# 24 of the 98 dense pairs placed beneath the final scatter, which waits for stored pairs once in seven chunks

## The reference

```python
def _egnn_conv(x, src, dst, edge_attr, W_msg, W_edge, W_root, b):
    msg = x[src] @ W_msg + edge_attr @ W_edge
    agg = jax.ops.segment_max(msg, dst, num_segments=x.shape[0])
    agg = jnp.where(jnp.isneginf(agg), 0.0, agg)
    return agg + x @ W_root + b
...
c1 = leaky_relu(_egnn_conv(X,  src, dst, edge_attr, W1_msg, W1_edge, W1_root, b1))
c2 = leaky_relu(_egnn_conv(c1, src, dst, edge_attr, W2_msg, W2_edge, W2_root, b2))
out = layernorm(x + c2)
```

## Time and profile before

| | |
|---|---|
| time, median of 2 runs | 1471.7 us (1471.67 to 1471.73) |
| the profiled execution's own time | 1473.16 us |
| its span | 1471.4 us |
| mean granted TensorE clock | 0.712 of 2.4 GHz |
| TensorE busy | 1008.0 us, 69% |
| VectorE busy | 803.4 us, 55% |
| ScalarE busy | 699.0 us, 48% |
| GpSimd busy | 989.6 us, 67% |

### The profile page before, as it was taken

The page is one execution under the profiler, slowest core; times in us unless marked ns, Lnnn a source line. Parts: engine busy times, 40 slices in busy tenths (PEclk is TensorE's granted clock), DMA queues, the critical chain, the costliest instruction groups (busy, mean ns, idle before and its releaser), DMA issues.

```text
span 1471.4 us, 16389 instructions
## 1 busy us (share of the span) xinstructions
PE 1008.0 (69%) x4312; PEld 665.1 (45%) x4312; DVE 803.4 (55%) x1736; ACT 699.0 (48%) x1711; POOL 989.6 (67%) x986
## 2 busy tenths in 40 slices
PE   3667677779999999988988898989898940000000
PEld 1333333346666666665655666656666630000000
DVE  3223332357777777777877888888888850000000
ACT  1223343346666666656666666666666660000000
POOL 4777777757777776467676767677765007777775
PEclk9787787785555555598988888889888865555555
DMA  7888798877776777666665666655666211111110
GB/s 208 258 271 271 210 293 286 273 223 219 206 219 202 218 205 216 207 186 174 168 168 166 168 172 176 171 165 153 178 175 170 86 41 34 34 34 32 34 34 26
DMA packets 106083, 247.72 MB, mean 168 GB/s; under 512 B 26664, under 2 KB 27729, under 8 KB 105992
## 3 DMA queue, kind: packets, MB, share of 16 engines
q1 hardware_dynamic: 67432, 161.21, 36.5%
q0 software_dynamic: 31360, 47.07, 13.7%
q10 hardware_dynamic: 7200, 38.40, 6.9%
HBM read 141.94 MB, written 105.80 MB: 168 GB/s over the span
## 4 chain that ended last, share of the span: by engine, by line
PE 35%; POOL 22%; issue 19%; DVE 11%; ACT 11%; DMA 1%; DVEq 0%; POOLq 0%; ACTq 0%; SPq 0%
PE ps L408 13%; PE ps_z L418 13%; POOL g_src L229 12%; POOL out L248 8%; ACT yo L555 5%; DVE yo L720 3%; PE ps_m L398 3%; DVE stat L731 3%; PE ps_t L394 2%; ACT c1d L640 2%; DVE rt L822 2%; POOL g_dst L229 2%; ACT nat L617 2%; PE ps_r L504 2%; PE ps_r L506 1%
## 5 line engine op out<-in xcount | busy, mean ns | idle before, releaser
L418 PEld LDWEIGHTS ps_z<-wr,c1t 97*128 97x128 f32 x1568 | 296.4, 272 | 103.3 <-issue 72.9
L408 PE MATMUL ps<-xtb,wr 97*96 97x512 f32 x392 | 300.4, 861 | 0.0
L418 PE MATMUL ps_z<-wr,c1t 97*128 97x96 f32 x1568 | 293.7, 352 | 2.9 <-DVE c1t L713 2.9
L248 POOL DMA_INDIRECT out<-nat,end_i x196 | 190.5, 972 | 136.6 <-DMA out<-yo 75.8
L229 POOL DMA_INDIRECT g_src<-agg_table,src_i x196 | 214.8, 1096 | 84.5 <-issue 54.3
L229 POOL DMA_INDIRECT g_dst<-in_x,own_i x196 | 189.2, 965 | 106.8 <-DVE nat L802 57.4
L239 POOL DMA_INDIRECT agg_table<-nat,all_i x196 | 206.3, 1053 | 72.9 <-issue 58.4
L555 ACT ACTIVATE yo<-yo,shift,rstd 128x96 f32<-128x96 f32 x680 | 253.0, 456 | 0.0
L229 POOL DMA_INDIRECT g_src<-in_x,src_i x196 | 188.0, 959 | 71.6 <-issue 58.8
L678 DVE TENSOR_TENSOR_SCAN mx<-mask,mx,ps_m 96x512 f32<-96x512 f32 x96 | 122.2, 1273 | 164.8 <-PE ps_m L398 164.8
L713 DVE TENSOR_TENSOR c1t<-ps,c1t 96x512 f32<-96x512 f32 x196 | 134.1, 684 | 75.0 <-ACT c1t L529 73.7
(11 more groups left out here) (57 smaller groups left out, 1172.5 us busy)
## 6 DMA issues: line engine op xcount, KB each, us to landing
xtb<-in_xt SPq DMA_DIRECT2D x98, 384.0 KB, 5.0
agg_table<-zero ACTq DMA_DIRECT2D x50, 750.0 KB
xn<-in_x SPq DMA_DIRECT2D x97, 384.0 KB, 3.3
out<-yo SPq DMA_DIRECT2D x97, 384.0 KB, 3.9
mask<-mask_row SPq DMA_DIRECT2D x98, 192.0 KB, 5.7
root_keep<-rt SPq DMA_DIRECT2D x49, 192.0 KB, 4.9
rt<-root_keep SPq DMA_DIRECT2D x49, 192.0 KB, 4.5
xe<-in_eat SPq DMA_DIRECT2D x98, 64.0 KB, 4.8
```

The lines of the kernel that those rows point to most:

```text
L248: nc.gpsimd.indirect_dma_start(out=rows, out_offset=bass.IndirectOffsetOnAxis(ap=end_i[:, t:t + 1], axis=0), in_=nat[:, t, :], in_offset=N ...
L408: nc.tensor.matmul(ps_1[0:D, h, :], wr1[:, :], xtb[:, k, half(h)], start=True, stop=True).then_inc(d_1, 1)
L418: last = nc.tensor.matmul(ps_z[:, h, row(j)], c1t[:, q % 2, cols(h * HJ + j)], wr2[:, :], start=True, stop=True)
```

## The change

- The 98 pairs are distributed anew: 6 in stage A as before, 35 in stage S (46 before), 33 in stage B (46 before), and 24 (`LATE` = 74 and up) in new loops behind stage B, on every engine that takes part. The late pairs normalise two of eight row blocks on VectorE.
- GpSimd no longer waits for all stores ahead of the final scatter. Once in GROUP = 7 chunks it loads a value from the last row of `pair_i` into a register: the number of pairs that must be stored so that all rows to which these seven chunks go are stored. It waits for the semaphore `s_stored` against that register.
- SyncE counts stored pairs into `s_stored`: after issuing the store of pair q it waits for the store of pair q - 1 to land and increments.
- The final scatter has no bounds check. It uses the index list of the table's scatter, which sends rows that are not a segment's last to rows of their own behind the output; `out` gets EP = 25088 more rows, cut off afterwards. `all_i` and the old `end_i` become one list, so one preparing operation goes (L657) and two are added for `pair_i`. GpSimd's start now waits for ten preparing operations, not nine.

```diff
-NS = 46
+NS = 35
+NM = 33
+GROUP = 7
...
-STEPS_B = spread(NQ - NA - NS, NCH, NA + NS)
+STEPS_B = spread(NM, NCH, NA + NS)
+LATE = NA + NS + NM
+STEPS_B[NCH] = range(LATE, LATE + 1)
+STEPS_B[NCH + 1] = range(LATE + 1, LATE + 2)
...
         def on_vector(q):
-            return VROWS if q < NA + NS else 0
+            return VROWS if q < NA + NS or q >= LATE else 0
...
             def scatter(rows, c, landed):
...
                         out=rows, out_offset=bass.IndirectOffsetOnAxis(ap=end_i[:, t:t + 1], axis=0),
-                        in_=nat[:, t, :], in_offset=None, bounds_check=N - 1,
-                        oob_is_err=False).then_inc(landed[c % 2], 16)
+                        in_=nat[:, t, :], in_offset=None).then_inc(landed[c % 2], 16)
...
-            pool.wait_ge(s_prep, 9)
+            pool.wait_ge(s_prep, 10)
...
-                scatter_maxima(c)
+                scatter(table, c, sc_t)
...
-            for k in range(YR):
-                pool.wait_ge(o_st[k], 16 * ((NQ + YR - 1 - k) // YR))
             for c in range(NCH):
+                if c % GROUP == 0:
+                    last = (c + GROUP) * TPC - 1
+                    pool.wait_ge(s_stored, nc.gpsimd.value_load(pair_i[P - 1:P, last:last + 1], min_val=1, max_val=NQ))
+                    pool.sem_inc(s_under, 1)
+                    pool.wait_ge(s_under, c // GROUP + 1)
                 pool.wait_ge(e_done, c + 1)
                 scatter(out, c, sc_o)
...
                 else:
                     sp.dma_start(out_tail, yo[0:TAIL, k, :]).then_inc(o_st[k], 16)
+                if q >= 1:
+                    stored(q - 1)
+
+            def stored(q):
+                sp.wait_ge(o_st[q % YR], 16 * (q // YR) + 16)
+                sp.sem_inc(s_stored, 1)
...
-            dense(range(NQ, NQ + 3))
+            dense(range(LATE, NQ + 3))
+            stored(NQ - 1)
...
                     last.then_inc(b_r, 1)
+            for d in range(LATE + 1, NQ + 1):
+                for h in range(2):
+                    dense(range(d, d + 1), h)
...
+            for d in range(LATE + 2, NQ + 2):
+                dense_head(range(d, d + 1))
+                dense_tail(range(d, d + 1))
             act.wait_ge(s_cleared, 16 * NZ)
...
-            V.scalar_tensor_tensor(out=end_i[:, :], in0=eq_c[:, :], scalar=float(FAR), in1=dst_i[:, :],
-                                   op0=ALU.mult, op1=ALU.add).then_inc(s_prep, 1)
...
+            V.tensor_scalar(pair_i[:, :], own_i[:, :], PN.bit_length() - 1, None,
+                            ALU.arith_shift_right).then_inc(s_prep, 1)
             dve.wait_ge(s_prep, 8)
-            V.tensor_tensor(all_i[:, :], aside_d[:, :], dst_i[:, :], ALU.add).then_inc(s_prep, 1)
+            V.tensor_tensor(end_i[:, :], aside_d[:, :], dst_i[:, :], ALU.add).then_inc(s_prep, 1)
+            V.tensor_scalar(pair_i[:, :], pair_i[:, :], 1, None, ALU.add).then_inc(s_prep, 1)
...
                 dense_tail(steps)
+            for d in range(LATE + 2, NQ + 2):
+                dense_head(range(d, d + 1))
+                dense_mid(range(d, d + 1))
+                dense_tail(range(d, d + 1))
```

More of the change, by code:

```diff
@@ L28 @@
 NA = 6
-NS = 46
+NS = 35
+NM = 33
 VROWS = 2
 AHEAD = 4
+GROUP = 7
+assert NCH % GROUP == 0
 assert N * D % (P * ZCOL) == 0 and NZ == NCH + 1 and NQ == 2 * NCH and (N - (NQ - 1) * PN) % J == 0
@@ L90, in gnn_kernel @@
         end_i = sb("end_i", [P, NT], i32)
-        all_i = sb("all_i", [P, NT], i32)
+        pair_i = sb("pair_i", [P, NT], i32)
         aside_i = sb("aside_i", [P, NT], i32)
@@ L151, in gnn_kernel @@
         o_st = sems("o_st", YR)
+        s_stored = sem("s_stored")
+        s_under = sem("s_under")
         sc_t = sems("sc_t", 2)
@@ L232, in gather @@
                     ).then_inc(landed[k], 16)
[L234 to L241, removed]
             def scatter(rows, c, landed):
@@ L348, in _ @@
             load_pair(1)
-            sp.wait_ge(s_prep, 9)
+            sp.wait_ge(s_prep, 10)
             sp.dma_start(mask_row, row_m[:, :]).then_inc(s_mask_w, 16)
@@ L482, in _ @@
                 else:
-                    dense(range(NQ, NQ + 1), 0)
-                    dense(range(NQ, NQ + 1), 1)
+                    dense(STEPS_B[c], 0)
+                    dense(STEPS_B[c], 1)
                 if c >= 1:
@@ L623, in _ @@
                     edge_std(c - 2)
-                steps = STEPS_B[c] if c < NCH else range(NQ + c - NCH, NQ + c - NCH + 1)
+                steps = STEPS_B[c]
                 dense_head(steps)
@@ L656, in _ @@
             V.tensor_scalar(row_m[:, :], row_m[:, :], 2.0, -1.0, ALU.mult, ALU.add).then_inc(s_prep, 1)
-            V.scalar_tensor_tensor(out=end_i[:, :], in0=eq_c[:, :], scalar=float(FAR), in1=dst_i[:, :],
-                                   op0=ALU.mult, op1=ALU.add).then_inc(s_prep, 1)
             V.tensor_scalar(own_i[:, :], dst_i[:, :], float(N - 1), None, ALU.min).then_inc(s_prep, 1)
             V.tensor_tensor(aside_d[:, :], aside_i[:, :], dst_i[:, :], ALU.subtract).then_inc(s_prep, 1)
-            dve.wait_ge(s_prep, 6)
+            dve.wait_ge(s_prep, 5)
             V.tensor_scalar(row_m[:, :], row_m[:, :], FMAX, None, ALU.mult).then_inc(s_prep, 1)
             V.tensor_tensor(aside_d[:, :], aside_d[:, :], eq_c[:, :], ALU.mult).then_inc(s_prep, 1)
+            V.tensor_scalar(pair_i[:, :], own_i[:, :], PN.bit_length() - 1, None,
+                            ALU.arith_shift_right).then_inc(s_prep, 1)
             dve.wait_ge(s_prep, 8)
-            V.tensor_tensor(all_i[:, :], aside_d[:, :], dst_i[:, :], ALU.add).then_inc(s_prep, 1)
+            V.tensor_tensor(end_i[:, :], aside_d[:, :], dst_i[:, :], ALU.add).then_inc(s_prep, 1)
+            V.tensor_scalar(pair_i[:, :], pair_i[:, :], 1, None, ALU.add).then_inc(s_prep, 1)
             dve.wait_ge(s_const, 9 * 16)
@@ L878 @@
         args[name] = nc.dram_tensor(f"in_{name}", a.shape, mybir.dt.from_np(a.dtype), kind="ExternalInput").ap()
-    out = nc.dram_tensor("out_0", (N, D), mybir.dt.float32, kind="ExternalOutput").ap()
+    out = nc.dram_tensor("out_0", (N + EP, D), mybir.dt.float32, kind="ExternalOutput").ap()
     gnn_kernel(nc, **args, out=out)
-    return run_bass_kernel_spmd(nc, [feed], core_ids=[0]).results[0]["out_0"]
+    return run_bass_kernel_spmd(nc, [feed], core_ids=[0]).results[0]["out_0"][0:N]
```

## The result

The changed kernel takes 1329.0 us (median of 2 runs, 1328.58 to 1329.41) against 1471.7: a ratio of 0.903, 95% interval 0.899 to 0.907. Four more runs of it beside the experiments gave 1328.6 us. The prediction was 1337 us, range 1320 to 1372.

The account below looks back on a forecast made before the run. GpSimd's list of indirect DMAs was taken to bind stages S, B and the final scatter: scatter start 1061 + 247 DMAs + 13 holds + 7 register waits + 8.5 end = 1336.5, plus 0.3, so 1337 us, range 1320 to 1372.

Parts of the forecast that it names:

- Stage S: 35 pairs instead of 46: GpSimd's scatter binds, first gather of stage B at 582.1, chunk 0 on VectorE at 591.
- Stage B: GpSimd's 360 gathers outlast the engines' list by 12 us; with 3 us of waits the final scatter starts at 1061.
- The term for VectorE's hold: In stage B, VectorE's work lengthens GpSimd's gathers by 0.85 us a pair, 28 us for 33 pairs.
- The 3 us for interlocking lists: In stage B, 3 us added for waits of GpSimd's list and the engines' list for one another.
- The engines' list: Stage B's 32 chunk intervals with a pair and 16 without: 492 us, so chunk 48 starts at 1083.
- The final scatter: Behind stage B: 196 DMAs of 1.26 us, 247 us, plus 13 us of losses beneath pairs and 7 of register waits.
- register waits: In the final scatter, seven register loads and waits on GpSimd cost 1.0 us each, 7 us.
- Group 6: Final scatter's group needing all 98 pairs: starts at 1292, no wait by 15 us; rival that it waits: 1364 us, chance 0.05.
- the prediction's estimate of 50 us by that page: In the final scatter, an exclusive port lock would charge 2.1 us for each of 24 late pairs; sum 1377.
- the lists did not interlock: Rival, stage B: GpSimd has no lead, chunks without a pair last 10.3 us, not 6.87; end at 1377, chance 0.14.
- The late pairs did not run at full clock: Rival, final scatter: late pairs take 5.03 us and cost GpSimd 1.24 each, +20, 1357 us; chance 0.12.
- Stage B's clock: Rival: TensorE's clock falls in stage B, at 1.2 GHz throughout 1577 us; chance 0.04.

Follow-up runs that it names:

- the early clears: The changed kernel with the clears of the table issued four chunks earlier on ScalarE's queue: 1319.4 us, ratio 0.897.

## Why the prediction was right, step by step

**The bound.** Right in mechanism. GpSimd's list of indirect DMAs binds from stage S on. It waits for nothing in stage B, the scatter follows the last gather at 0.30 us, and the early clears moved the end by what they took out of the list.

**Stage S.** First gather at 580.2 (582.1 predicted), chunk 0 on VectorE at 587.7 (591). The landing behind the last scatter DMA took 1.5 us instead of 3.9.

**Stage B.** The last gather ended at 1050.7 and the scatter started at 1051.0, where 1061 was predicted. That is the whole error of the sum: 1336.8 us for a span of 1326.5. The time was missed by only 8 us because a second error stood against it: the prediction put 0.3 us between span and time, from the span of one run and the median of two, but a run takes 1.7 to 2.2 us more than its own span (1473.16 and 1471.4 before, 1328.58 and 1326.5 after). The term for VectorE's hold was 28 us; 361.1 us for 360 gathers at 0.944 leave 21. The 3 us for interlocking lists were not needed. A loss per pair was the wrong unit besides: the kernel with 21 pairs in stage B lost 19.6 us and that with 40 pairs 28.4. Put down to the operation that ends 0.81 to 0.85 us ahead of each lengthened DMA, the 21 us of the changed kernel are 11.3 for the 33 pairs and 10.0 for the chunks' own L817 and L797; with 21 pairs it is 12.7 and 6.8, so 12 fewer pairs saved nothing there. The engines' list was sized well: chunk 48 at 1088.4 (1083).

**The final scatter.** 266.9 us, where 267 was predicted, but from other parts, so that the sum came out was luck. Predicted: 247 of bare DMAs, 13 of holds (10 beneath the late pairs, 3 ahead of them), 7 of register waits. Measured: 247, and 204.7 - 196 x 0.958 = 17 of holds (11.6 beneath the late pairs, 5.3 ahead of them), 0 of register waits, 3 of the odd gap. The late pairs ran at 6.72 us after the first few, as forecast, at a granted clock of 0.53, and then cost 0.41 us each. But the additions of the last pair of stage B and of the first three late ones came 5.1 to 7.5 us apart and cost 1.0 to 1.34 us each, the dearest above the 1.24 of the earlier trace rows. What a hold costs depends on where in the addition the DMA starts. At 6.72 us the two keep in step: from the start of an addition to that of the fifth DMA behind the held one it is 0.94 + 0.83 + 0.30 + 4 x 1.26 = 7.1 us, about 0.4 us into the next addition, where the held DMAs of the earlier trace rows start too. That is an estimate from these rows; it gives the 0.4 us a pair again.

**Group 6.** The last store was issued at 1269.6 and counted as landed at 1272.1, and group 6 started at 1282.8, as in this row, without a wait:

```profile
1282.82 0.96 POOL L247 DMA_INDIRECT out<-nat,end_i  x1 [0.30 <-issue]
```

Predicted: landed at 1277, start at 1292. The slack of 15 us is some 11, and 12 more late pairs used it up and more.

**Wrong in it.** The step "VectorE's L720 and L731, 2.1 us together, lengthen the scatter DMA" (lines of the kernel before). Of the two only the addition, L720, does. The Trainium skill ("SBUF — State Buffer", on the shared port pair) excludes a VectorE operation with at most one SBUF input from the contention, outside the 2-port modes, so the prediction's estimate of 50 us by that page should not have counted the statistics. With the addition alone it would have been 24 x 0.94 = 23 us; 11.6 were measured beneath the late pairs. And the register waits were put at 7 us and cost nothing.

**The rivals.** Chunks without a pair took 7.1 to 8.4 us, not 10.3: the lists did not interlock. The late pairs did not run at full clock (granted 0.53, with TensorE busy for 165 of 175 us). Group 6 didn't wait. Stage B's clock was 0.88 up to the last gather, not lower than before but a little higher.

## What to carry to other kernels

When one engine's list of DMAs runs through all stages, add up that list alone, from its first wait to its last issue, and look at what it waits for; other engines' work costs only where it makes that list wait or slows its instructions. A coarse wait at the end ("all stores") and a split of work that is to hide beneath it belong together: here the finer wait alone gained 80 us, the split alone lost 60, and both gained 143. Before a slowdown is laid to two operations that always run back to back, take one of them away.

## What the runs showed of the hardware

- VectorE operations with two inputs, all in SBUF, hold an indirect DMA that GpSimd is issuing. If the DMA starts beneath one, it ends 0.81 to 0.85 us after the operation does (128x768, 0.94 us; 96x512, 0.69 us; 128x384, 0.56 us). The one of 0.94 us also holds a DMA that started up to about 0.6 us before it. 0.96 us become up to 2.37. Operations with an operand in PSUM (128x384, 0.56 us) and bn_stats hold none, and an addition of 0.24 us (128x96) lengthened DMAs by less than 0.1 us.
- Register loads and waits on GpSimd's queue between DMAs, 49 of them, added nothing measurable to a list of back-to-back DMAs (1327.6 us beside 1328.6 with seven).
- The unchecked scatter DMA took 0.958 us at the median, the bounds-checked one 0.972.
